# The experts' second product as three products of rounded parts, in a Perceiver, Mamba and expert block on one Trainium2 core

## What is computed

```
hidden = layernorm(x)                      # 512 tokens of 256
gathered = hidden.reshape(-1, 256)[top_idx.T]            # (8, 512, 256)
h = gelu(einsum('ecd,edf->ecf', gathered, W1) + b1[:, None, :])   # (8, 512, 1024)
out_e = einsum('ecf,efd->ecd', h, W2) + b2[:, None, :]            # (8, 512, 256)
w = combine_weights[tok, e_ids]
out = zeros_like(x).at[tok.reshape(-1)].add((out_e * w[..., None]).reshape(-1, 256))
```

## Time and profile before

| | |
|---|---|
| median of 3 runs | 774.5 us (774.43 to 775.55) |
| the profiled execution's own time | 774.9 us |
| its span, first to last instruction | 773.2 us |
| mean granted TensorE clock | 0.985 |
| busy TensorE, VectorE, ScalarE, GpSimd | 737.1, 516.1, 404.8, 402.0 us |
| the expert stage, first product to last output | about 695.8 to 773.2 us |

### The profile page before, as it was taken

One profiled execution on the slowest core, in us unless ns is written; L12 is line 12 of the kernel. 1 busy time (PEld: TensorE's weight loads), 2 busy tenths in 40 slices (PEclk: granted clock), 3 DMA queues, 4 the chain that ended last, 5 costly groups with the idle time before them and its releaser, 6 DMA issues.

```text
span 773.2 us, 14596 instructions
## 1 busy us (share of the span) xinstructions
PE 737.1 (95%) x5539; PEld 681.3 (88%) x5539; DVE 516.1 (67%) x1117; ACT 404.8 (52%) x1079; POOL 402.0 (52%) x355
## 2 busy tenths in 40 slices
PE   8999999999999999999999999999999886999996
PEld 8889999999989999999989899999999762568885
DVE  7666575567574776888778678976698887840102
ACT  2534454454355566655566566456656553734331
POOL 6517117102700299658747986687397978730000
PEclk9999999999999999999999999999999995999998
DMA  8642110011001200310211012000100107604800
GB/s 310 238 148 49 62 26 1 1 62 26 1 8 55 53 15 1 102 26 16 68 34 27 14 59 63 14 15 2 32 14 22 28 22 240 245 1 125 286 27 30
DMA packets 51418, 49.62 MB, mean 64 GB/s; under 512 B 19524, under 2 KB 46352, under 8 KB 50320
## 3 DMA queue, kind: packets, MB, share of 16 engines
q1 hardware_dynamic: 51344, 48.64, 20.7%
HBM read 44.10 MB, written 4.52 MB: 63 GB/s over the span
## 4 chain that ended last, share of the span: by engine, by line
PE 65%; POOL 15%; issue 9%; DVE 7%; ACT 3%; DMA 1%; POOLq 0%; DVEq 0%; SPq 0%; ACTq 0%
PE psum L1733 16%; PE psum L1698 16%; PE psum L1714 5%; POOL work L629 4%; PE psum L2154 4%; PE psum L2144 4%; PE psum L1667 3%; POOL y_sum L642 3%; POOL work L636 3%; PE psum L1674 2%; PE psum L2016 2%; PE psum L1764 2%; PE psum L1792 1%; PE psum L1608 1%; PE psum L1648 1%
## 5 line engine op out<-in xcount | busy, mean ns | idle before, releaser
L1347 ACT ACTIVATE pt_hi<-psum 128x512 fp32r<-128x512 f32 (+1 forms) x192 | 87.2, 489 | 201.9 <-PE psum L1714 148.4
L1733 PE MATMUL psum<-kvn_hi,pt_hi 128*128 128x256 f32 x512 | 150.1, 293 | 0.0
L1733 PE MATMUL psum<-kvn_hi,pt_lo 128*128 128x256 f32 x512 | 144.3, 282 | 0.0
L1733 PE MATMUL psum<-kvn_lo,pt_hi 128*128 128x256 f32 x512 | 144.2, 282 | 0.0
L1049 DVE TENSOR_REDUCE rowmax<-psum 128x1 f32<-128x728 f32 x64 | 58.6, 915 | 61.9 <-PE psum L1698 61.7
L1733 PEld LDWEIGHTS psum<-kvn_lo,pt_hi 128*128 128x128 f32 x512 | 97.3, 190 | 0.2
L1733 PEld LDWEIGHTS psum<-kvn_hi,pt_hi 128*128 128x128 f32 x512 | 97.1, 190 | 0.2
L1733 PEld LDWEIGHTS psum<-kvn_hi,pt_lo 128*128 128x128 f32 x512 | 97.1, 190 | 0.0
L1698 PE MATMUL psum<-kvt_hi,qk_hi 128*128 128x364 f32 (+1 forms) x384 | 90.5, 344 | 0.0
L903 DVE TENSOR_TENSOR pt_lo<-psum,pt_hi 128x512 fp32r<-128x512 f32 x128 | 82.0, 683 | 8.9 <-ACT pt_hi L1347 8.8
L1698 PE MATMUL psum<-kvt_hi,qk_lo 128*128 128x364 f32 (+1 forms) x384 | 84.5, 328 | 0.0
(11 more groups left out here) (251 smaller groups left out, 1570.9 us busy)
## 6 DMA issues: line engine op xcount, KB each, us to landing
w<-in_L_ffn_W_dram SPq DMA_DIRECT2D x16, 1024.0 KB, 8.5
ctx_nat<-in_ctx_dram SPq DMA_DIRECT2D x8, 1024.0 KB, 5.0
bc<-dbc_keep SPq DMA_DIRECT2D x48, 128.0 KB, 4.5
q_cur<-q_keep SPq DMA_DIRECT2D x14, 128.0 KB, 3.0
q_keep<-q_t SPq DMA_DIRECT2D x1, 1536.0 KB, 6.0
wq_sb<-in_L_xattn_Wq_dram SPq DMA_DIRECT2D x1, 1024.0 KB, 9.9
wk_nat<-in_L_xattn_Wkv_dram SPq DMA_DIRECT2D x1, 1024.0 KB, 11.9
wv<-in_L_xattn_Wkv_dram SPq DMA_DIRECT2D x1, 1024.0 KB, 14.7
```

What stands on the lines that cost most here:

```text
L1347: act.activation(pt_hi[u][:, t0:t1, :], where[:, 0:(t1 - t0) * P].rearrange("p (t m) -> p t m", m=P), ACT.Copy)\
L1733: pe.matmul(PV, w[u][:, j, :], x_[slot][:, j, :], start=(j == 0 and w is pt_hi and x_ is kvn_hi), stop=False)
```

## The change

The second product of the first round becomes, for each f, three float32r matmuls: hid_hi x w2_hi, hid_hi x w2_lo, hid_lo x w2_hi. The parts are made during the stage:

- ScalarE rounds w2 to w2_hi in four pieces of 128x512 (`weight_highs`): for expert 0 two pieces when the last w_out of the Mamba part is done and two behind the last f_hi; for expert e + 1 between the gelus of e and o_hi of e.
- GpSimd subtracts: w2_lo = w2 - w2_hi, four pieces of 128x512 for each expert (`weight_lows`), each as its high piece is there.
- VectorE casts hid[f] to hid_hi[f] and subtracts, hid_lo[f] = hid[f] - hid_hi[f], 128x128 each, as each gelu is done.
- TensorE waits for hid_lo per f and for w2_lo per two f, and no longer for all eight gelus.

w2_hi and w2_lo have two sets each, 32 KB in each partition, placed over Mamba buffers that are dead by then. The activation that loads the gelu table reads another source for this reason. To free semaphores, three of the start (s_psc, s_xhl, s_plo) are now one, s_lat, and f_ct and f_cte are counted in f_b2 and f_b2e; what waits for what stays the same there.

```diff
+        PARTS = FT // 2
+        over = ExitStack()
+        w2_hi = [[sb(over, f"w2_hi{i}_{n}", [P, 2 * C], F32R) for n in range(PARTS)] for i in range(2)]
+        w2_lo = [[sb(over, f"w2_lo{i}_{n}", [P, 2 * C], F32R) for n in range(PARTS)] for i in range(2)]
+        over.close()
...
+        hid_hi = sb(mam, "hid_hi", [P, FT, P], F32R)
+        hid_lo = sb(mam, "hid_lo", [P, FT, P], F32R)
...  GpSimd
+            def weight_lows():
+
+                for e in range(E):
+                    src = w2[e % RING][:].rearrange("p f c -> p (f c)")
+                    if e >= 2:
+                        pool.wait_ge(f_o, e - 1)
+                    for n in range(PARTS):
+                        pool.wait_ge(f_wh, PARTS * e + n + 1)
+                        pool.tensor_tensor(w2_lo[e % 2][n][:], src[:, n * 2 * C:(n + 1) * 2 * C],
+                                           w2_hi[e % 2][n][:].bitcast(F32), ALU.subtract).then_inc(f_ws, 1)
+
+            weight_lows()
...  VectorE, expert_round
+                        for f in range(FT if isinstance(r, int) else 0):
+                            dve.wait_ge(f_he, FT * e + f + 1)
+                            dve.tensor_copy(hid_hi[:, f, :], hid[:, f, :]).then_inc(f_hh, 1)
+                            dve.wait_ge(f_hh, FT * e + f + 1)
+                            dve.tensor_tensor(hid_lo[:, f, :], hid[:, f, :], hid_hi[:, f, :].bitcast(F32),
+                                              ALU.subtract).then_inc(f_hs, 1)
                         dve.wait_ge(f_o, e + 1)
...  ScalarE
+            def weight_highs(e, first, final):
+
+                act.wait_ge(ld_e[e % RING], 32 * (e // RING + 1))
+                if e >= 2:
+                    act.wait_ge(f_o, e - 1)
+                src = w2[e % RING][:].rearrange("p f c -> p (f c)")
+                for n in range(first, final):
+                    act.activation(w2_hi[e % 2][n][:], src[:, n * 2 * C:(n + 1) * 2 * C], ACT.Copy).then_inc(f_wh, 1)
...
-                    act.activation(warm_out[:], a_neg[:, 0, 0:1], ACT.Gelu_apprx_tanh)
+                    act.activation(warm_out[:], ident[:, 0:1], ACT.Gelu_apprx_tanh)
...
+                        if isinstance(r, int) and e + 1 < E:
+                            weight_highs(e + 1, 0, PARTS)
                         act.wait_ge(f_os, e + 1)
                         act.activation(o_hi[:], o_s[:], ACT.Copy).then_inc(f_oh, 1)
...
             for t in range(TT):
+                if t == INLINE:
+                    act.wait_ge(v_yo, INLINE + 1)
+                    weight_highs(0, 0, PARTS // 2)
                 act.wait_ge(f_ln, t + 1)
                 act.activation(f_hi[:, t, :], f_nat[t], ACT.Copy).then_inc(f_hi_done, 1)
+            weight_highs(0, PARTS // 2, PARTS)
             expert_round(0)
...  TensorE, expert_round
-                        pe.wait_ge(f_he, FT * (e + 1))
+                        if not isinstance(r, int):
+                            pe.wait_ge(f_he, FT * (e + 1))
...
                         for f in range(FT):
-                            last = pe.matmul(psum[:, 4 + i % 2, 0:C], hid[:, f, :], w2[i][:, f, :],
-                                             start=(f == 0), stop=(f == FT - 1))
+                            where = psum[:, 4 + i % 2, 0:C]
+                            if not isinstance(r, int):
+                                last = pe.matmul(where, hid[:, f, :], w2[i][:, f, :], start=(f == 0), stop=(f == FT - 1))
+                                continue
+                            pe.wait_ge(f_hs, FT * e + f + 1)
+                            if f % 2 == 0:
+                                pe.wait_ge(f_ws, PARTS * e + f // 2 + 1)
+                            cols = slice(f % 2 * C, (f % 2 + 1) * C)
+                            for w, x_ in ((hid_hi, w2_hi), (hid_hi, w2_lo), (hid_lo, w2_hi)):
+                                last = pe.matmul(where, w[:, f, :], x_[i % 2][f // 2][:, cols],
+                                                 start=(f == 0 and w is hid_hi and x_ is w2_hi),
+                                                 stop=(f == FT - 1 and w is hid_lo))
```

More of the change, by code:

```diff
@@ L250, in perceiver_kernel @@
         s_dve, s_pool, s_act = sem("s_dve"), sem("s_pool"), sem("s_act")
-        s_psc, s_xhl, f_rs = (sem(n) for n in ("s_psc", "s_xhl", "f_rs"))
-        s_id, s_pstat, s_pln, s_platt, s_pevac, s_pq, s_pqe, s_pwk, s_pwke, s_plo = (sem(n) for n in (
-            "s_id", "s_pstat", "s_pln", "s_platt", "s_pevac", "s_pq", "s_pqe", "s_pwk", "s_pwke", "s_plo"))
+        s_lat, f_rs = (sem(n) for n in ("s_lat", "f_rs"))
+        s_id, s_pstat, s_pln, s_platt, s_pevac, s_pq, s_pqe, s_pwk, s_pwke = (sem(n) for n in (
+            "s_id", "s_pstat", "s_pln", "s_platt", "s_pevac", "s_pq", "s_pqe", "s_pwk", "s_pwke"))
         s_cmv, s_csh, s_cz, s_cn, s_khi, s_klo, s_qcur = (sem(n) for n in (
@@ L279, in perceiver_kernel @@
             "idx tab oh cnt val pre pos b1 b1e").split())
-        (f_stat, f_ln, f_hi_done, f_lo_done, f_hl, f_ct, f_cte, f_pick, f_turn, f_turned, f_cs, f_cse, f_gat,
-         f_gate, f_h, f_he, f_o, f_os, f_oh, f_ol, f_sc, f_sce, f_b2, f_b2e, f_shift, f_all, f_fin, f_done) = (
+        (f_stat, f_ln, f_hi_done, f_lo_done, f_hl, f_pick, f_turn, f_turned, f_cs, f_cse, f_gat,
+         f_gate, f_h, f_he, f_hh, f_hs, f_wh, f_ws, f_o, f_os, f_oh, f_ol, f_sc, f_sce, f_b2, f_b2e, f_shift, f_all, f_fin, f_done) = (
             sem("f_" + n) for n in (
-                "stat ln hi lo hl ct cte pick turn turned cs cse gat gate h he o os oh ol sc sce b2 b2e shift all "
+                "stat ln hi lo hl pick turn turned cs cse gat gate h he hh hs wh ws o os oh ol sc sce b2 b2e shift all "
                 "fin done").split())
@@ L561, in _ @@
             link(pool.tensor_scalar(lvar[:], lmv[:, :, 1], 1.0 + EPS, EPS * EPS, ALU.mult, ALU.add))
-            pool.tensor_tensor(lscale[:], lvar[:], mhalf[:, 0:TT], ALU.pow).then_inc(s_psc, 1)
+            pool.tensor_tensor(lscale[:], lvar[:], mhalf[:, 0:TT], ALU.pow).then_inc(s_lat, 1)
             def latent_parts():
                 pool.wait_ge(s_pln, TT)
-                pool.tensor_scalar(x_hi[:], x_lat[:], 1.0, 0.0, ALU.mult, ALU.add).then_inc(s_xhl, 1)
-                pool.wait_ge(s_xhl, 1)
-                pool.tensor_tensor(x_lo[:], x_lat[:], x_hi[:].bitcast(F32), ALU.subtract).then_inc(s_xhl, 1)
+                pool.tensor_scalar(x_hi[:], x_lat[:], 1.0, 0.0, ALU.mult, ALU.add).then_inc(s_lat, 1)
+                pool.wait_ge(s_lat, 2)
+                pool.tensor_tensor(x_lo[:], x_lat[:], x_hi[:].bitcast(F32), ALU.subtract).then_inc(s_lat, 1)
             def ctx_norm(b):
@@ L1282, in expert_round @@
                     dve.wait_ge(f_sce, CK * (EG * r + q + 2))
-            dve.wait_ge(f_b2e, CK)
+            dve.wait_ge(f_b2e, CK + 1)
             dve.sem_inc(f_sce, CK)
@@ L1538, in side_job @@
                 elif job == E:
-                    act.wait_ge(f_ct, 1)
-                    act.activation(coef_t[:], psum[0:E, JB, :], ACT.Copy).then_inc(f_cte, 1)
+                    act.wait_ge(f_b2, 1)
+                    act.activation(coef_t[:], psum[0:E, JB, :], ACT.Copy).then_inc(f_b2e, 1)
                 else:
-                    act.wait_ge(f_b2, job - E)
+                    act.wait_ge(f_b2, job - E + 1)
                     act.activation(acc_t[:, job - E - 1, :], psum[:, JB, :], ACT.Copy).then_inc(f_b2e, 1)
@@ L2036, in side_job @@
                         last = pe.transpose(psum[0:E, JB, t * P:(t + 1) * P], coef[:, t, :], ident[:])
-                    last.then_inc(f_ct, 1)
+                    last.then_inc(f_b2, 1)
                 else:
@@ L2040, in side_job @@
                     if k == 0:
-                        pe.wait_ge(f_cte, 1)
+                        pe.wait_ge(f_b2e, 1)
                         pe.wait_ge(ld_b2, 16)
                     else:
-                        pe.wait_ge(f_b2e, k)
+                        pe.wait_ge(f_b2e, k + 1)
                     pe.matmul(psum[:, JB, :], b2_sb[:, k * P:(k + 1) * P], coef_t[:], start=True, stop=True)\
@@ L2086, in _ @@
                 if n == NS - 2:
-                    pe.wait_ge(f_b2e, CK)
+                    pe.wait_ge(f_b2e, CK + 1)
                     pe.wait_ge(f_lo_done, 1)
                     gather(1, 1, 0)
-            pe.wait_ge(f_b2e, CK)
+            pe.wait_ge(f_b2e, CK + 1)
             pe.wait_ge(f_lo_done, 1)
```

8 lines of the change are left out of this document (4 added, 4 removed).

## The result

The changed kernel takes 786.16 us (median; 785.84 to 786.87), the kernel before on the same chip 774.98 (774.43 to 775.55): a ratio of 1.0149, 95% interval 1.0133 to 1.0165. The change is slower by 11.2 us between the medians; 786.4 was forecast. The profiled execution has a span of 784.2 us against 773.2, at a mean granted clock of 0.972 against 0.985.

What follows compares the result with a forecast made beforehand. TensorE, busy 95% of 773.2 us, bounds the kernel. VectorE and GpSimd holding each other up adds 7.5 to 15.4, plus 0.4 at the start; middle 11.9 on 774.9, less 0.4, gives 786.4 us, range 776 to 796.

Steps and rivals of the forecast that it cites:

- TensorE's gain: Expert stage: 24 rounded products take 2.82 us per expert, gaining 0.63 us each; stage 6.4 us shorter if parts are ready.
- as meant: Rival: the parts made by other engines never hold TensorE up, giving 768.1 us; chance 0.09.
- ScalarE at nothing: ScalarE's four weight roundings per expert, 0.631 us each, fit in the period and were costed at nothing.
- GpSimd's duration and start: Four weight subtractions per expert, 1.31 us each with the gap, starting 4.65 us after the period's start.
- One VectorE operation per GpSimd operation: Beside GpSimd, VectorE gets one operation through per GpSimd operation, 1.3 us, whatever its own length.
- The pair: VectorE's cast plus subtraction of 128x128 per f, with two hops of 0.03: 0.565 us (0.52 to 0.62).
- Four left: Experts 1, 2, 3, 6: four VectorE operations remain when GpSimd starts, period 10.43 us against 7.96, +2.47; three give +1.16.
- The even period: Experts 1, 2, 3 and 6 were each counted alike, at +2.47 us, or +1.16 with one VectorE operation fewer remaining.
- The third rival: Slower than forecast: stalls lower TensorE's clock, 1 to 4 us per expert, or VectorE stretches GpSimd; 792 to 810 us; chance 0.10.
- Experts 0, 4, 7 and the entry: Separate terms: +2.7 (or +1.4), +0.1 (or -1.2), -0.6, and 0.4 us for f_lo held up at the stage's start.
- A sign of being wrong that came: Listed as showing error: short casts and subtractions, TensorE waiting for w2_lo or ScalarE's roundings, or granted clock below 1.00.
- Half blocked: Rival: two VectorE operations pass per gap, or fp32 casts don't wait; experts alternate, 780 us (777 to 782); chance 0.15.

Runs made afterwards that it cites:

- the kernel with two fillers: The changed kernel with two idle 128x128 identity products on TensorE ahead of the waits of f = 5, 6, 7 in experts 0 to 6; 784.59 us, ratio 1.0134.

## Why the prediction was right, and where it was luck

- **TensorE's gain: right.** 24 products in 2.85 us (forecast 2.82). The kernel without low parts gives 768.0; "as meant" was 768.1.
- **ScalarE at nothing: right.** 0.62 us for each rounding; TensorE waits for no w2_hi and no w2_lo.
- **GpSimd's duration and start: right.** 1.31 us, from 4.63 us after the period's start (forecast 1.31 and 4.65) in experts 2 and 5, whose first products ran at the full clock; from 5.7 to 6.5 us in experts 1, 3 and 6, where they didn't.
- **One VectorE operation per GpSimd operation: right**, and the step that decided. The four of expert 2 that last 1.25 to 1.33 us beside GpSimd's four show it, and the run without GpSimd's operations, in which none is held.
- **The pair: mis-sized, 0.463 us and not 0.565.** The cast (0.220) and the subtraction (0.293) were as estimated; of the two hops of 0.03 one is there, and in place of the other the next cast starts 0.08 before the subtraction ends. The Trainium skill (VectorE: DVE Perf Modes, the errata section) gives the cast, as an estimate, as 0.127 us by its formula and 0.223 by the measured fixed part: the 0.220 us here agree with the second.
- **Four left: the step that failed.** With the true pair, from 1.35 to 4.64 us there are 7.1 pairs, and one or two operations are left, as the kernel with two fillers has it. The forecast's working then gives 7.3 to 7.8 us for experts 1, 2, 3 and 6, not 10.43. Where four were caught (experts 2 and 5), VectorE started late: GpSimd's low parts from the expert before still held o_lo or the first cast, so that six and nine operations were left. From expert 0 to 6 there were 3, 0, 6, 0, 1, 9 and 0 left, where the forecast had four in most. I had that reach only in expert 5, since a period of 10.43 covers GpSimd's work, and a shorter one does not. Expert 5 I had at +3.3; it is +4.5.
- **The even period: wrong.** Experts 1, 2, 3, 6 were to add 2.47 each (or 1.16); they add 1.01, 3.60, 1.25 and 0.47. Behind the stalls of experts 0, 2 and 5 the clock had fallen; the slow product there delays the gelus, so nothing is caught in that expert, and also GpSimd, which then reaches into the next. The third rival had the clock's fall, 1 to 4 us each time; 4.6 in three places came true. That a slow expert is also one with few catches was in neither.
- **Experts 0, 4, 7 and the entry:** +1.46 (2.7 or 1.4), +0.25 (0.1), -0.62 (-0.6), +0.8 (0.4). Expert 0 had three left.
- **A sign of being wrong that came:** among what would show it wrong the forecast had a granted clock below 1.00, and 0.83 and 0.66 were seen. Its own sum had the clock at no loss, and only the third rival had a term for it.
- **"Half blocked", 780:** its premise, casts that don't wait, is refuted by the run in which GpSimd only writes. Its picture of alternating experts, a short one whose GpSimd work hurts the next, was nearer the trace than my even one.

So the sum, 11.9 forecast and 11.2 measured between the medians, has the right cause, VectorE held up by GpSimd, but its nearness is partly luck: too long a pair stood in for a reach of GpSimd and a fall of the clock that I hadn't counted.

## What to carry to other kernels

Work moved to an idle GpSimd isn't free for VectorE: find the VectorE operations that fall into GpSimd's busy stretches, count each at GpSimd's duration, and ask which of them TensorE waits for. With 17 caught the changed kernel was 11 us slower than before, with 18 caught the run with the later GpSimd 3 to 4 us. Few large operations leave less to do when GpSimd starts (here from 786 to 772 us by merging alone). Ask not only what is left when the other engine starts, but also where its work ends in the next period. Where an otherwise busy TensorE stalls for a microsecond or two, have a term for the next product at the lower clock too: here it came behind some stalls and not behind others.

## What the runs showed of the hardware that was not expected

- A VectorE cast beside a GpSimd operation that only writes takes up to 1.374 us; a subtraction of two SBUF inputs beside the same takes at most 0.296.
- Behind one idle gap of 1.8 us, in a stage at 1.00, the granted clock was 0.82 and 0.84 in two stretches of 5 us; with products in the gap it was 1.00 in both. Behind idle gaps of 1.80 and 2.64 us in two other kernels it stayed at 1.00.
- Alternating casts and subtractions of 128x128, where each subtraction waits for its cast, follow each other at 0.463 us a pair, less than the 0.513 of their two durations.
- Four times the columns cost a cast less than twice the time: 0.220, 0.294 and 0.428 us for 128, 256 and 512; the subtraction takes 0.293, 0.426 and 0.693.
